# Transposing two neighbouring tokens as one 32-bit word ahead of a channel-attention gram

## What is computed

```
xt = gn(x).reshape(b, c, n).transpose(0, 2, 1)        # n = 2304 tokens
q, k, v = split(xt @ w_qkv, 3)                        # heads of d = 24 channels
q = q / max(sqrt(sum over tokens of q*q), EPS)        # the same for k
attn = softmax(einsum('bhpn,bhnq->bhpq', k * temperature, q))
out = einsum('bhnp,bhpq->bhnq', v, attn) @ w_out + b_out
x = x + out (back as b, c, H, W)
```

## Time and profile before

| | |
|---|---|
| median of 3 runs | 464.36 us (461.95 to 465.39) |
| profiled execution, span | 460.6 us |
| PE busy | 362.6 us (79%) |
| PEld busy | 241.1 us (52%) |
| DVE busy | 318.2 us (69%) |
| ACT busy | 258.6 us (56%) |
| POOL busy | 161.2 us (35%) |
| mean granted TensorE clock | 0.924 |

### The profile page before, as it was taken

How to read it: one execution, slowest core, us unless ns; L and a number is a source line. 1 busy time by engine, 2 the same in 40 slices (tenths; PEclk the granted TensorE clock), 3 DMA queues, 4 the chain that set the end, 5 groups by cost and what they waited for, 6 DMA issues and landing times.

```text
span 460.6 us, 10784 instructions
## 1 busy us (share of the span) xinstructions
PE 362.6 (79%) x3772; PEld 241.1 (52%) x3772; DVE 318.2 (69%) x762; ACT 258.6 (56%) x392; POOL 161.2 (35%) x116
## 2 busy tenths in 40 slices
PE   0125674899879984899989985899889988997696
PEld 0024534675557552674567553664567556754443
DVE  4699832898589853798499852898499848366454
ACT  1073558771987286762987194843996298721200
POOL 0066138312761076202841174202940285112000
PEclk9997975899999997999899996999899989999789
DMA  8996200003891188404980388305870462035246
GB/s 290 307 309 177 53 1 0 1 2 109 273 305 38 74 247 272 135 4 134 278 308 3 108 259 261 99 2 173 288 260 3 134 205 75 2 119 185 76 140 204
DMA packets 30698, 68.07 MB, mean 148 GB/s; under 512 B 5361, under 2 KB 11825, under 8 KB 30641
## 3 DMA queue, kind: packets, MB, share of 16 engines
q1 hardware_dynamic: 30352, 66.86, 46.3%
q10 hardware_dynamic: 288, 0.46, 0.3%
HBM read 29.55 MB, written 28.31 MB: 126 GB/s over the span
## 4 chain that ended last, share of the span: by engine, by line
PE 44%; DVE 16%; issue 16%; ACT 13%; POOL 6%; DMA 2%; SPq 1%; ACTq 1%; DVEq 0%; POOLq 0%
PE u_ps L908 23%; PE g_ps L908 8%; PE s_ps L908 7%; POOL l_sb L435 6%; ACT h_sb L499 5%; ACT xn L493 4%; DVE bnst L677 2%; ACT tok L517 2%; DMA x_sb<-in_x_dram 2%; DVE xn L706 2%; ACT mh L544 2%; PE u_ps L954 1%; SPq L355 1%; PE u_ps L955 1%; PE s_ps L1025 1%
## 5 line engine op out<-in xcount | busy, mean ns | idle before, releaser
L435 POOL TENSOR_TENSOR l_sb<-xn,h_sb 128x768 f16<-128x768 f32 x72 | 120.3, 1686 | 66.5 <-ACT h_sb L499 59.5
L908 PE MATMUL g_ps<-tok 128*128 128x64 f16 (+1 forms) x864 | 90.0, 244 | 27.9 <-ACT tok L517 16.1
L832 DVE SCALAR_TENSOR_TENSOR x_sb<-u_ps,bias,x_sb 128x384 f32 (+1 forms) x144 | 82.5, 611 | 22.9 <-PE u_ps L908 21.9
L517 ACT COPY tok<-u_ps 128x768 f16<-128x768 f16 x104 | 78.6, 806 | 25.2 <-PE u_ps L957 24.9
L908 PEld LDWEIGHTS g_ps<-tok 128*128 128x128 f16 x864 | 58.6, 100 | 57.4 <-ACT tok L517 15.7
L908 PE MATMUL u_ps<-h_sb,ml 128*128 128x384 f16 (+1 forms) x336 | 79.6, 347 | 8.2 <-DVE x_sb L832 8.2
L499 ACT ACTIVATE h_sb<-x_sb,rb 128x768 f16 (+1 forms) x72 | 72.8, 1020 | 20.2 <-DVE rb L729 20.2
L677 DVE BATCH_NORM_STATS2 bnst<-x_sb 128x6 f32 (+2 forms) x120 | 68.0, 622 | 7.2 <-DMA x_sb<-in_x_dram 7.0
L493 ACT ACTIVATE xn<-x_sb,rb 128x768 f32 (+1 forms) x63 | 63.5, 1018 | 10.5 <-DVE rb L729 8.7
L954 PE MATMUL u_ps<-id,h_sb 128*128 128x128 f16 x288 | 50.5, 228 | 18.1 <-POOL l_sb L435 13.7
L955 PE MATMUL u_ps<-id,l_sb 128*128 128x128 f16 x288 | 50.9, 229 | 7.3 <-issue 7.3
(11 more groups left out here) (145 smaller groups left out, 634.3 us busy)
## 6 DMA issues: line engine op xcount, KB each, us to landing
x_sb<-in_x_dram SPq DMA_DIRECT2D x48, 384.0 KB, 5.3
out_dram<-x_sb SPq DMA_DIRECT2D x48, 384.0 KB, 2.7
x_sb<-in_x_dram SPq DMA_DIRECT2D x48, 192.0 KB, 5.5
out_dram<-x_sb SPq DMA_DIRECT2D x48, 192.0 KB, 2.8
hl<-h_sb SPq DMA_DIRECT2D x48, 96.0 KB, 2.5
hl<-l_sb SPq DMA_DIRECT2D x48, 96.0 KB, 2.6
h_sb<-in_groups_dram ACTq DMA_DIRECT2D x1, 384.0 KB, 4.7
w<-in_L_conv_w_qkv_dram SPq DMA_DIRECT2D x1, 288.0 KB
```

The costliest lines, as they stand in the source:

```text
L435: nc.gpsimd.tensor_tensor(l_sb[:, par, t, cols], xn[:, c % XN_RING, :], h_sb[:, par, t, cols], ALU.subtract).then_inc(l_ok, 1)
L517: nc.scalar.copy(tok[:, j % TOK_RING, :, :].rearrange("p b n -> p (b n)"), slot_ps(j)).then_inc(tok_a, 1)
L832: V.scalar_tensor_tensor(out=xs, in0=block_ps(n), scalar=bias[:, t:t + 1], in1=xs, op0=ALU.add, op1=ALU.add).then_inc(out_ok, 1)
L908: return nc.tensor.matmul(dst, lhs, rhs, start=start, stop=stop, skip_group_check=True)
```

## The change

Two neighbouring tokens of one channel are two fp16 values that lie side by side in `h_sb` or `l_sb`; they are now read as one 32-bit word (`words_of`). A pair of slots (256 tokens, a "twin" J) is transposed in two halves: half k = 2J takes the words of the high part, half k = 2J+1 those of the low part, each in three fp32 transposes of 128 words against a 128 x 128 fp32 identity (`transpose`). `half_ps` and `half_tok` are the 2 x 192 words of a half in PSUM and in `tok`, which now has three places for a twin, each with 384 channels (high and low) by two tokens. `to_tok` copies a half where it copied a slot, with the same 18 copies on the same engines at the same places of their orders, and waits for the gram three twins back. `gram` takes a twin: for each of the two tokens of a word, e, and each image, the same three products as before, whose operands step through `tok` by two elements. Two twins are transposed ahead (`PAIR_AHEAD`); within gram(J) the transposes of twin J+2 stand one behind each product of 384 columns, four in all, and two behind the last product. `gram` is called behind each odd j, ahead of the small step of that j.

```diff
--- before.py
+++ after.py
@@ -33,10 +33,10 @@
 GN_EPS = 1e-5
 NORM_EPS = 1e-12
 NX = 3
-TOK_RING = 4
+TOK_RING = 3
+PAIR_AHEAD = 2
 RING = 4
 LOAD_LAG = 2
-AHEAD = 3
 XN_RING = 3
 GN_COL = 400
 
@@ -114,6 +114,7 @@
     C1 = C - P
     PAIRS = B // 2
     SLOTS = N // P
+    TWINS = SLOTS // 2
     HC = C // 2
     NH = HEADS // 2
     GROUPS = 3
@@ -147,7 +148,7 @@
         l_sb = sb("l_sb", [P, 2, 3, N], F16)
         hl = sb("hl", [P, 2, N], F16)
         xn = sb("xn", [P, XN_RING, GW])
-        tok = sb("tok", [P, TOK_RING, 2, 384], F16)
+        tok = sb("tok", [P, TOK_RING, 2, 384, 2], F16)
         w0 = sb("w0", [P, 3 * C])
         w1 = sb("w1", [P, 3 * C])
         wh0 = sb("wh0", [P, 2 * C], F16)
@@ -164,7 +165,7 @@
         grp = sb("grp", [P, 6, P], BF16)
         mask = sb("mask", [HC, HC])
         mask16 = sb("mask16", [HC, HC], F16)
-        id32 = sb("id32", [HC, HC])
+        id32 = sb("id32", [P, P])
         ones = sb("ones", [P, 3], F16)
         minus_half = sb("minus_half", [P, 1])
         bias = sb("bias", [P, 3])
@@ -218,9 +219,16 @@
         u_ps = ctx.enter_context(nc.psum_tensor("u_ps", [P, RING, 512], F32))
         z_ps = s_ps[:, 1, 0:C].bitcast(F16)
 
-        def slot_ps(j):
-
-            return u_ps[:, j % RING, 0:384].bitcast(F16)
+        def half_ps(k):
+
+            return u_ps[:, k % RING, 0:2 * C].rearrange("p (b n) -> p b n", b=2)
+
+        def half_tok(k):
+
+            words = tok[:, k // 2 % TOK_RING, :, :, :].rearrange("p b n e -> p b (n e)").bitcast(F32)
+            return words[:, :, C * (k % 2):C * (k % 2) + C]
+
+        words_of = [a[:, :, :, :].rearrange("p q t n -> p (q t n)").bitcast(F32) for a in (h_sb, l_sb)]
 
         def block_ps(n):
 
@@ -513,9 +521,8 @@
             def to_tok(q, j):
 
                 act.wait_ge(tr_mm, q * SLOTS + j + 1)
-                need(act, gram_mm, q * SLOTS + j + 1 - TOK_RING)
-                nc.scalar.copy(tok[:, j % TOK_RING, :, :].rearrange("p b n -> p (b n)"), slot_ps(j)
-                               ).then_inc(tok_a, 1)
+                need(act, gram_mm, q * TWINS + j // 2 + 1 - TOK_RING)
+                nc.scalar.copy(half_tok(j), half_ps(j)).then_inc(tok_a, 1)
 
             def spread_norms(q):
 
@@ -546,7 +553,7 @@
 
             def small_gram(q):
 
-                act.wait_ge(gram_mm, (q + 1) * SLOTS)
+                act.wait_ge(gram_mm, (q + 1) * TWINS)
                 for b in (0, 1):
                     nc.scalar.copy(e16[:, b, :], g_ps[:, b, G_C:512]).then_inc(e_ok, 1)
 
@@ -630,7 +637,7 @@
                 dve.wait_ge(c_group, 32)
                 V.tensor_copy(grp[:, :, :].rearrange("p a m -> p (a m)"), st_grp)
                 V.tensor_copy(id16[:, :], st_id)
-                V.tensor_copy(id32[:, :], st_id[0:HC, 0:HC]).then_inc(set_v, 1)
+                V.tensor_copy(id32[:, :], st_id).then_inc(set_v, 1)
 
             def high_constants():
 
@@ -732,9 +739,8 @@
             def to_tok(q, j):
 
                 dve.wait_ge(tr_mm, q * SLOTS + j + 1)
-                need(dve, gram_mm, q * SLOTS + j + 1 - TOK_RING)
-                V.tensor_copy(tok[:, j % TOK_RING, :, :].rearrange("p b n -> p (b n)"), slot_ps(j)
-                              ).then_inc(tok_v, 1)
+                need(dve, gram_mm, q * TWINS + j // 2 + 1 - TOK_RING)
+                V.tensor_copy(half_tok(j), half_ps(j)).then_inc(tok_v, 1)
 
             def norms(q):
 
@@ -746,7 +752,7 @@
 
                 dve.wait_ge(r8_ok, q + 1)
                 V.tensor_tensor(dq[:, :, :], r8[:, 4:8].unsqueeze(2).to_broadcast([HC, 4, HC]),
-                                id32[:, :].unsqueeze(1).to_broadcast([HC, 4, HC]), ALU.mult).then_inc(dq_ok, 1)
+                                id32[0:HC, 0:HC].unsqueeze(1).to_broadcast([HC, 4, HC]), ALU.mult).then_inc(dq_ok, 1)
                 V.tensor_tensor(rk[:, :], r8[:, 0:4], temp4[:, :], ALU.mult).then_inc(rk_ok, 1)
 
             def softmax_in(q):
@@ -937,42 +943,51 @@
                 else:
                     pe.wait_ge(tok_a, q * NA + j - before + 1)
 
-            def transposes(q, par, j):
-                if j < RING:
-
-                    need(pe, out_ok, (q - 1) * NO + NO - RING + j + 1)
+            def transpose(q, par, k, i):
+
+                J, low = k // 2, k % 2
+                if i == 0:
+                    if k < RING:
+
+                        need(pe, out_ok, (q - 1) * NO + NO - RING + k + 1)
+                    else:
+
+                        in_tok(q, k - RING)
+                    if J * 2 * P % GW == 0:
+                        pe.wait_ge(l_ok if low else h_ok, q * NC_ + 3 * (J * 2 * P // GW) + 3)
+                t = (0, 2, 1)[i]
+                src = words_of[low][:, (par * 3 + t) * (N // 2) + P * J:(par * 3 + t) * (N // 2) + P * J + P]
+                dst = half_ps(k)
+                main, tail = (C1, 0) if low else (0, P)
+                if t != 1:
+                    nc.tensor.transpose(dst[:, t // 2, main:main + P], src, id32[:, :])
                 else:
-
-                    in_tok(q, j - RING)
-
-                if j * P % GW == 0:
-                    pe.wait_ge(h_ok, q * NC_ + 3 * (j * P // GW) + 3)
-                    pe.wait_ge(l_ok, q * NC_ + 3 * (j * P // GW) + 3)
-                bank = slot_ps(j).rearrange("p (b n) -> p b n", b=2)
-                px = slice(P * j, P * j + P)
-                for b in (0, 1):
-                    nc.tensor.transpose(bank[:, b, 0:P], h_sb[:, par, 2 * b, px], id16[:, :])
-                    nc.tensor.transpose(bank[:, b, 256:384], l_sb[:, par, 2 * b, px], id16[:, :])
-                nc.tensor.transpose(bank[:, :, P:P + C1], h_sb[:, par, 1, px], id16[:, :])
-                nc.tensor.transpose(bank[:, :, P + C1:P + 2 * C1], l_sb[:, par, 1, px], id16[:, :]).then_inc(tr_mm, 1)
-
-            def gram(q, j):
-                in_tok(q, j)
-                if j == 0:
+                    nc.tensor.transpose(dst[:, :, tail:tail + C1], src, id32[:, :]).then_inc(tr_mm, 1)
+
+            def gram(q, par, J):
+                in_tok(q, 2 * J)
+                in_tok(q, 2 * J + 1)
+                if J == 0:
 
                     need(pe, tl_ok, 3 * q)
                     need(pe, pf_ok, 3 * q)
-                first, end = j == 0, j == SLOTS - 1
-                for b in (0, 1):
-                    s = tok[:, j % TOK_RING, b, :]
-                    bank = g_ps[:, b, :]
-
-                    mm(bank.rearrange("p (r c) -> p r c", r=2)[:, :, 0:C], s[:, 0:P], s[:, 0:384], first)
-
-                    mm(bank[:, G_C:G_C + C1], s[:, P:256], s[:, P:C], False)
-
-                    last = mm(bank[:, G_B:G_B + C1], s[:, 256:384], s[:, P:C], False)
+                ahead = [(k, i) for k in (2 * (J + PAIR_AHEAD), 2 * (J + PAIR_AHEAD) + 1) for i in range(3)]
+                for e in (0, 1):
+                    for b in (0, 1):
+                        s = tok[:, J % TOK_RING, b, :, e]
+                        bank = g_ps[:, b, :]
+
+                        mm(bank.rearrange("p (r c) -> p r c", r=2)[:, :, 0:C], s[:, 0:P], s[:, 0:384], J == 0 and e == 0)
+                        if J + PAIR_AHEAD < TWINS:
+                            transpose(q, par, *ahead.pop(0))
+
+                        mm(bank[:, G_C:G_C + C1], s[:, P:256], s[:, P:C], False)
+
+                        last = mm(bank[:, G_B:G_B + C1], s[:, 256:384], s[:, P:C], False)
                 last.then_inc(gram_mm, 1)
+                if J + PAIR_AHEAD < TWINS:
+                    for k, i in ahead:
+                        transpose(q, par, k, i)
 
             def finish_gram(q):
 
@@ -1145,13 +1160,12 @@
                     transpose_wv()
                 more, small, norm_next = loop or p + 1 < PAIRS, not first, loop or p + 2 < PAIRS
                 if more:
-                    for j in range(AHEAD):
-                        transposes(p + 1, 1 - par, j)
+                    for k in range(2 * PAIR_AHEAD):
+                        for i in range(3):
+                            transpose(p + 1, 1 - par, k, i)
                 for j in range(SLOTS):
-                    if more:
-                        gram(p + 1, j)
-                        if j + AHEAD < SLOTS:
-                            transposes(p + 1, 1 - par, j + AHEAD)
+                    if more and j % 2:
+                        gram(p + 1, 1 - par, j // 2)
                     for what in hooks(p, FIRST_PE_A, PE_A, LAST_PE_A, PAIRS - 1).get(j, ()):
                         if what == "sums":
                             if norm_next:
```

## The result

| | before | after |
|---|---|---|
| median of 4 runs each | 463.44 us (461.95 to 465.39) | 471.44 us (469.36 to 472.11) |
| profiled execution, span | 460.6 us | 469.9 us |
| mean granted TensorE clock | 0.924 | 0.941 |

The ratio is 1.0173, 95% interval 1.0132 to 1.0215. The forecast was 463 with a range of 453 to 474: the range holds the time, the call (no change the likeliest) does not. The clock is no part of it, being higher than before.

The account below looks back on a forecast made before the run. TensorE's own work was 44% of the chain, no engine the bound everywhere. First stage -0.4, two stall rounds -0.3 each, five stages 0: span 460.6 - 1.0 = 459.6, plus 3.8 to the median: 463, range 453 to 474.

Parts of the forecast that it names:

- rivals at 473: Strided weight loads in the gram, +10 (chance 0.12); or granted clock dropping once a stage, +1.5 a stage (0.07).
- the one on the copies: Stage A's 18 copies: ScalarE 4.2 us a stage freed; mid-stage, the 0.3 wait for GpSimd goes; copy 17 0.33 shorter.
- More gates go: Rival: ScalarE's freed 4.2 us a stage brings softmax or stall 1 us sooner a stage: 456, chance 0.11.
- 32-bit transposes at two cycles a column: TensorE, stage A: a transpose of 128 columns costs 107 ns at 2.4 GHz, bounds 56 and 213.
- The rivals of one and of four cycles: Transpose cost per column: one cycle gives 455, -8 in all (chance 0.12); four cycles give 486 (chance 0.03).
- The rivals of 473 and 491, by the step: Two-element operand step: slower weight loads, +10, 473 (chance 0.12); moving operand at half rate, 491 (chance 0.06).
- ScalarE 480, VectorE unchanged: Stage A's copies of 384 words: ScalarE 480 ns instead of 806, VectorE still 545, bounds 0.2 below to 0.03 above.
- Gate of gram(3) as before: First gate behind the exponential: two short copies end at 137.38, where one long copy did; moving over 0.5 breaks it.
- From the gate to the folded weights 7.5: Stage A's middle: gram(3) at 137.4, four pairs at 1.60, `v` 1.1, folded weights at 144.9 (-0.1); 7.65 before.
- Tail: Behind the folded weights: copy 17 ends at +3.65, gram(8) runs +3.7 to +4.6, against 4.48 before (+0.1).
- Clock the same: Granted clock of stage A stays at full; the rival, a drop once a stage, gives 473, chance 0.07.
- Stage A ends where it did: End of stage A unchanged in five such stages: 0 us.

Follow-up runs that it names:

- e5: Kernel before plus two GpSimd waits: part 6 behind VectorE's diagonal product, part 8 behind the attention's masked products; 461.53 us, ratio 1.0001.
- e6: Kernel before with 384-word copies and both GpSimd waits (parts 6 and 8); 453.58 us, ratio to before 0.9817.
- e12: e6 with the gram taken by pairs of slots, still packed fp16 transposes and operands; 461.65 us, ratio to before 0.9954.
- e4: Changed kernel plus two GpSimd waits: part 6 behind the diagonal product, part 8 behind the attention's masked products; 458.84 us, ratio to before 0.9877.
- e1: Kernel before with only the copies changed, to 384 32-bit words instead of 768 halves; 464.05 us, ratio to before 0.9999.
- e8: e4 with all six transposes of a pair behind the gram's products instead of four between them; 455.80 us, ratio to before 0.9778.
- e3: Changed kernel plus one wait: GpSimd's part 8 starts only after the attention's masked products; 461.30 us, ratio to before 0.9965.

## Why the prediction was wrong

The medians form one ladder. Before 463.4; the waits, 461.5 (not told from 463.4 by its ratio); short copies, 453.6 (-8); gram by pairs, fp16 transposes, 461.7 (+8.1); 32-bit ones with their order and rings instead, 458.8 (-2.8); the waits taken away, 471.4 (+12.6). (By the ratios, in 464 us: 0, -8.5, +6.4, -3.6, +13.7, each known to some 2 us.)

The traces have a second gauge, the distances between the exponentials (`ez`) of neighbouring pairs. The first is 47.76 us before (88.32 to 136.08) and 50.63 after (88.03 to 138.66). Two of the seven distances hold an instruction stall. They are 54.4 and 54.5 before, 54.6 and 54.4 after, and scatter from 50.3 to 55.8 over all profiles, so no loss can be read there. The sum of the other five, from one profile of each kernel:

| before | e5, waits | e6, and short copies | e12, and pairs | e4, the change with waits | after | e1, short copies alone |
|---|---|---|---|---|---|---|
| 228.5 | 226.7 | 222.9 | 228.0 | 229.3 | 240.5 | 233.1 |

The short copies by themselves lose 4.6 us here (before to e1; nothing by the medians), and the changed kernel 12.0. For e4 and e8 the profiled execution was one of their slower ones (461.45 and 457.57 us), so their sums are the least sure. Three readings agree in sign on both gauges: the short copies gain once the collisions are out (8.0 by the medians, 3.8 here), the grain loses (8.1 and 5.1), and the collisions that the waits remove cost the most (12.6 and 11.2). The 32-bit transposes are not told from nothing: a gain of 2.8 by the medians, a loss of 1.2 here. So the loss has two causes, the collisions and the grain, and one gain against them, the short copies. The forecast held copies, grain and transposes together at -1.0; they come to -2.7 by the medians (461.5 to 458.8), -5.7 by the ratios and +2.6 over the five distances (226.7 to 229.3), so the runs neither bear out the -1.0 nor refute it. The collisions it did not have.

That the time lies in the forecast's range is luck: 474 was set by rivals at 473 that fell, and not by what happened.

**The step that failed** is the one on the copies: "In the middle, copies 6 to 8 end earlier, the high part behind them too, and the 0.3 wait for GpSimd goes." That is true as far as it goes, but it follows the high part only forward to TensorE. What starts on GpSimd behind that high part is a subtraction of 1.65 us, and the step never asks what VectorE does at that time. With it failed the silent assumption that the softmax chain is as long as before: from the first transposes to the exponential it took 8.00 (128.08 to 136.08) and now takes 10.16 (128.50 to 138.66). Of these 2.2 us, 0.7 lie ahead of `dq`; `dq` takes 1.9 more but `rk` 1.45 less; VectorE then waits 0.5 for the products that need `dq`, and `lz` times `rk` takes 0.4 more. The warning was in the trace of before: `rk`, four elements a partition, at 1.60 us. None of the rivals was this one. "More gates go" began at the same place, the time that ScalarE gets free, and had the wrong sign. One more step was right only as a sum: that the short copies give at the gates and in the tail what the grain of two slots takes there. Each of the two terms is 4 to 8 us (e6, e12).

Point by point:

- *32-bit transposes at two cycles a column*: right. 0.11 apart at full clock (the last fence of this list), against 107 ns forecast. The rivals of one and of four cycles fall.
- *Loads hidden but for 0.08 a pair, pair at 1.60*: right, 1.62.
- *The step of two costs nothing*: right. Twelve products take 1.08 against 1.05 in the kernel before and 1.06 in e12, and a pair took 1.62. The rivals of 473 and 491, by the step, fall.
- *ScalarE 480, VectorE unchanged*: right, 476 and 543. That they shorten nothing, since the gate then wants two copies and the last product two slots, was forecast as one sum; it holds (e5 461.5, e12 461.7), but as two terms that cancel. I had not seen the first of them, 1.0 a stage to be had without the grain (e6).
- *Gate of gram(3) as before*: right against the exponential, 1.10 behind its start where it was 1.30. From the first transposes it moved by 2.0 (9.30 to 11.26), beyond the 0.5 that the prediction named as a sign of being wrong.
- *From the gate to the folded weights 7.5*: measured 9.05 (139.76 to 148.81). Between the last transposes and `v` lie 1.5 us of waiting for `ax`; in e3, which has `ax` short again, it is 7.60 (136.09 to 143.69).
- *Tail*: right. gram(8) starts 3.71 behind the folded weights (forecast 3.7), after an idle piece of 0.92 (forecast 1.1).
- *Clock the same*: right over the span, not in this step. The windows (busy us by engine, clock, DMA share, GB/s), after:
```profile
128.50:130.50 2.00, 2.00 (x12) 2.00 (x11) 0.94 (x2) 2.00 (x4) 2.00 (x3) 0.50 0.85 298
```
  and before:
```profile
128.00:129.70 1.70, 1.26 (x20) 1.01 (x18) 1.27 (x3) 1.07 (x3) 1.70 (x2) 1.00 1.00 398
```
  The first transposes ran at 1.2 GHz, 0.21 apart, and VectorE's first copy came 1.68 behind their start where it was 0.97: 0.7 of the 2.2 us by which the exponential is late here. Two neighbours here and two at 338 us, after:
```profile
128.98 0.42 PE L965 MATMUL u_ps<-id,h_sb 128*128 128x128 f32 x1
129.19 0.64 PE L963 MATMUL u_ps<-id,l_sb 128*128 128x128 f32 x2
...
338.62 0.27 PE L965 MATMUL u_ps<-id,h_sb 128*128 128x128 f32 x1
338.73 0.38 PE L963 MATMUL u_ps<-id,l_sb 128*128 128x128 f32 x2
```
  Counted from the folding (`mh`) of the pair before, `dq` starts no later than it did (31.28 against 31.42), so in this step the 0.7 is not lost: stage A starts that much earlier against the pair before.
- *Stage A ends where it did*: wrong, 24.9 us after its start (128.50 to 153.44) against 21.4. Of the 3.5, 2.2 lie before the exponential, 1.2 between it and the folded weights, 0.1 in the tail. From exponential to exponential the step grew by less, 2.9.

## What to carry to other kernels

When an engine off the critical path gets faster, follow its next steps one by one to where they land in time, and check what each engine that shares a port with them does there: a shorter copy on ScalarE moved a subtraction on GpSimd into two instructions of VectorE. Read the durations of fixed shapes in the groups by form first; one that varies from 0.5 to 4 us already collides, and placing the other engine's work (a wait, or one step later in the order) is an edit of a few lines that gave back more here (12.6 us) than the change cost (8.0). On the kernel before it gave nothing that can be told; there it made room for the short copies. And a coarser grain of hand-over has a price at each gate, even if the work itself costs the same.

## What the runs showed of the hardware

- A VectorE instruction with two SBUF operands does not slow down beside a GpSimd subtraction, it stands: `dq` of 96 x 384 took 0.54 us alone. In another stretch of the kernel before it took 4.61: it began while five subtractions ran back to back, and ended at 83.50, 0.41 behind their end (83.09). No gap between two of them let it in. The rows, with those of GpSimd first:
```profile
75.06 8.03 POOL L435 TENSOR_TENSOR l_sb<-xn,h_sb 128x768 f16<-128x768 f32 x5
...
78.89 4.61 DVE L748 TENSOR_TENSOR dq<-r,id 96x384 f32<-96x384 f32 x1
...
179.16 0.54 DVE L748 TENSOR_TENSOR dq<-r,id 96x384 f32<-96x384 f32 x1
```
  GpSimd's subtraction kept its mean, 1686 ns before and 1694 after: in this kernel it is VectorE that pays.
- Added waits made the kernel faster: two semaphore waits on GpSimd took 471.4 to 458.8.
- An fp32 transpose of 128 columns, with a weight load of its own, follows a product or another transpose at 0.11 us at full clock.
- ScalarE's copy out of PSUM follows the elements and not the bytes: 806 ns for 768 halves, 476 for 384 words of the same bytes. VectorE's does not gain (545 and 543).
